# Graph attention layer on one core: the last two x products behind their s, the first R row from a TensorE product, four adj pieces loaded early, the verdict from a bound

## What is computed

```python
Wh = x @ W.T                               # 8192 x 256
s_i = Wh @ r[:256, 0];  s_j = Wh @ r[256:, 0]
e = s_i[:, None] + s_j[None, :]            # 8192 x 8192
e = where(e >= 0, e, 0.2 * e)
e = where(adj == 0, -inf, e)
out = gelu(softmax(e, axis=1) @ Wh)        # exact gelu
return layernorm(x + out)                  # over the 256 features
```

## Time and profile before

| | us |
|---|---|
| median of three runs | 1577.04 |
| profiled execution | 1579.86 |
| its span in the trace | 1578.1 |
| PE busy | 1547.4 (98%) |
| DVE busy | 1482.8 (94%) |
| ACT busy | 1180.9 (75%) |
| POOL busy | 455.3 (29%) |
| mean granted clock of PE | 0.992 |

### The profile page before, as it was taken

The page is one execution under the profiler, slowest core; times in us unless marked ns, Lnnn a source line. Parts: engine busy times, 40 slices in busy tenths (PEclk is TensorE's granted clock), DMA queues, the critical chain, the costliest instruction groups (busy, mean ns, idle before and its releaser), DMA issues.

```text
span 1578.1 us, 37090 instructions
## 1 busy us (share of the span) xinstructions
PE 1547.4 (98%) x12693; PEld 1536.3 (97%) x12693; DVE 1482.8 (94%) x1853; ACT 1180.9 (75%) x1527; POOL 455.3 (29%) x660
## 2 busy tenths in 40 slices
PE   9969999999999999999999999999999999999996
PEld 8869999999999999999999999999999999999996
DVE  4789999999999999999999999999999999999996
ACT  5666687777777777877777777777777777777773
POOL 0022223332232323223232322333232233333220
PEclk9989999999999999999999999999999999999998
DMA  7466876958777696878768686877878687787860
GB/s 175 99 95 80 109 99 81 139 75 125 100 115 105 86 134 81 125 94 121 99 91 129 87 123 89 127 94 98 121 93 123 84 126 95 102 115 99 114 91 29
DMA packets 295267, 164.41 MB, mean 104 GB/s; under 512 B 12336, under 2 KB 291120, under 8 KB 295216
## 3 DMA queue, kind: packets, MB, share of 16 engines
q0 software_dynamic: 278976, 142.12, 68.5%
q1 hardware_dynamic: 16240, 21.80, 4.9%
HBM read 289.67 MB, written 8.42 MB: 189 GB/s over the span
## 4 chain that ended last, share of the span: by engine, by line
PE 95%; issue 3%; ACT 1%; DMA 0%; POOL 0%; POOLq 0%; DVE 0%; ACTq 0%
PE acc L653 30%; PE acc L643 30%; PE acc L646 30%; PE acc L616 3%; PE acc L604 1%; ACT gates L341 0%; PE acc L582 0%; DMA R_row<-w_rows 0%; ACT P_hi L417 0%; ACT WV_hi L335 0%; DMA w_rows<-w_in 0%; POOL adj_in L249 0%; PE acc L592 0%; POOL rstd L286 0%; POOLq L58 0%
## 5 line engine op out<-in xcount | busy, mean ns | idle before, releaser
L643 PE MATMUL acc<-WV_hi,P_hi 128*128 (+1 forms) x4096 | 999.0, 282 | 9.8 <-ACT P_hi L417 9.7
L646 PE MATMUL acc<-WV_lo,P_hi 128*128 (+1 forms) x4096 | 998.1, 281 | 0.0
L643 PEld LDWEIGHTS acc<-WV_hi,P_hi 128*128 128x128 f32 x4096 | 774.8, 189 | 10.5 <-ACT P_hi L417 10.2
L417 ACT CAST P_hi<-Pw 128x1024 fp32r<-128x1024 f32 x512 | 537.5, 1050 | 316.4 <-DVE Pw L501 163.1
L646 PEld LDWEIGHTS acc<-WV_lo,P_hi 128*128 128x128 f32 x4096 | 772.8, 189 | 0.0
L501 DVE SCALAR_TENSOR_TENSOR Pw<-R_row,X,gatesT 128x512 f32<-128x512 f32 x1024 | 711.5, 749 | 2.8 <-DMA R_row<-w_rows 2.8
L511 DVE TENSOR_TENSOR P_lo<-Pw,P_hi 128x1024 fp32r<-128x1024 f32 x512 | 626.7, 1224 | 41.3 <-ACT P_hi L417 39.0
L249 POOL DMA_DIRECT2D adj_in<-in_adj x512 | 330.6, 653 | 873.9 <-ACT gates L341 820.1
L653 PE MATMUL acc<-WV_hi,P_lo 128*128 (+1 forms) x4096 | 575.7, 283 | 0.0
L341 ACT ACTIVATE gates<-adj_in 128x1024 uint8<-128x1024 bf16 x512 | 537.4, 1050 | 34.5 <-DMA adj_in<-in_adj 26.5
L653 PEld LDWEIGHTS acc<-WV_hi,P_lo 128*128 128x128 f32 x4096 | 527.1, 189 | 0.0
(11 more groups left out here) (63 smaller groups left out, 200.8 us busy)
## 6 DMA issues: line engine op xcount, KB each, us to landing
adj_in<-in_adj POOLq DMA_DIRECT2D x512, 256.0 KB, 5.2
out<-y SPq DMA_DIRECT2D x64, 128.0 KB, 6.1
y<-in_x POOLq DMA_DIRECT2D x60, 128.0 KB, 5.9
Pw<-in_x SPq DMA_DIRECT2D x48, 128.0 KB, 3.6
R_row<-w_rows SPq DMA_DIRECT2D x16, 256.0 KB, 6.5
x_res<-in_x SPq DMA_DIRECT2D x20, 128.0 KB, 2.7
w_in<-in_L_gnn_W SPq DMA_DIRECT2D x1, 256.0 KB, 3.2
w_rows<-w_in SPq DMA_DIRECT2D x1, 32.0 KB, 2.1
```

The lines of the kernel that those rows point to most:

```text
L417: nc.scalar.copy(P_hi[:, u % 2], Pw[u][:]).then_inc(s_hi, 1)
L643: nc.tensor.matmul(acc[r_][:, v, 0:HC], P_hi[:, u % 2, par, bass.ts(v, P)], WV_hi[:, k, :], start=(first and u == 0 and par == 0), stop=False)
L646: nc.tensor.matmul(acc[r_][:, v, 0:FOUT], P_hi[:, u % 2, par, bass.ts(v, P)], WV_lo[:, k, :], start=False, stop=False)
```

## The change

The first stage does 30 whole products (0 to 29) and all 32 transposes. Of the rows 30 and 31 PE first computes only the two columns of s (`s_product`, a product of 2 columns instead of 258) and later the 256 columns of Wh (`late_product`). ACT takes V of these from S, and makes their `WV_hi` after the factor R (two parts) and within the first two groups (two parts). DVE makes their `WV_lo` in pieces 1 to 4 of the first row block, and the last column of `WV_hi` in piece 5; PE waits for them before the block's last piece.

The first R row isn't read back from DRAM. DVE multiplies the 32 x 32 unit matrix by s_i of the first 512 rows (`spread`, 32 x 512), PE multiplies this by a 32 x 128 tile of ones, which puts the row s_i on all partitions, DVE cuts it at `neg_M` out of PSUM, and ACT takes its exponential. The rows for the other blocks go through DRAM as before, and the first of them to be loaded is that of the second block.

POOL issues the loads of pieces 0 and 1 earlier (at `s_xT` 4 and 8), and those of pieces 2 and 3 still in the x stage, when the first and the second piece are gated. ACT gates pieces 0 and 1 in the x stage (after products 8, 10, ... 22), and nothing in the first piece of the main stage. DVE transposes the first piece's gates after product 18.

The verdict takes the largest |Wh| from products 0 to 27, and for the rest a bound: the largest |x| of the last two loads times the sum of |W| per output. It moves from DVE to POOL (a second partition reduction and ten small instructions). `applies` runs the main stage first and waits for the flag behind it; the general path still reads the flag.

The diff, cut to its core:

```diff
...
+        red = sb("red", [P, 6])
+        top = sb("top", [P, 6])
+        x_max = sb("x_max", [P, 2])
...
-        fits = sb("fits", [P, 5])
+        fits = sb("fits", [P, 6])
...
+        ones = y[0:32, 0, 0:P]
+        spread = y[0:32, 2:4, :].rearrange("p u (g n) -> p (u g) n", n=32)
+        ps_s = [acc[0][:, j, 0:4] for j in range(2)]
+        ps_row = acc[0][:, 0, :]
+        ps_Rt = acc[0][0:NC, 1, 0:P]
...
+            body()
             eng.wait_ge(s_flag, 1)
-            flag = eng.value_load(taken[0:1, 0:1], min_val=0, max_val=1)
-            with eng.If(flag == 1):
-                body()
...
-            load_rows(0, 0)
-            sp.wait_ge(s_Rld[0], 16)
...
-            pool.wait_ge(s_xT, 10)
+            pool.wait_ge(s_xT, 4)
             load(0, 0, 0, 0)
-            pool.wait_ge(s_xT, 18)
+            pool.wait_ge(s_xT, 8)
             load(0, 0, 0, 1)
-            pool.wait_ge(s_red, 2)
-            nc.gpsimd.partition_all_reduce(top[:, 0:2], red[:, 0:2], P, REDUCE_MAX).then_inc(s_top, 1)
-            pool.wait_ge(s_red, 3)
-            nc.gpsimd.partition_all_reduce(top[:, 2:3], red[:, 2:3], P, REDUCE_MAX).then_inc(s_top, 1)
+            pool.wait_ge(s_gate, GP)
+            load(0, 0, 1, 0)
+            pool.wait_ge(s_gate, 2 * GP)
+            load(0, 0, 1, 1)
+            pool.wait_ge(s_red, 4)
+            nc.gpsimd.partition_all_reduce(top[:, 0:1], red[:, 0:1], P, REDUCE_MAX).then_inc(s_top, 1)
+            pool.wait_ge(s_red, 5)
+            nc.gpsimd.partition_all_reduce(top[:, 1:6], red[:, 1:6], P, REDUCE_MAX).then_inc(s_fit, 1)
+            pool.wait_ge(s_fit, 1)
+            nc.gpsimd.tensor_scalar(fits[:, 0:1], top[:, 0:1], top[:, 1:2], MAX_SPREAD, ALU.add, ALU.is_le).then_inc(s_fit, 1)
+            nc.gpsimd.tensor_scalar(fits[:, 1:3], top[:, 0:2], MAX_S, None, ALU.is_le).then_inc(s_fit, 1)
+            nc.gpsimd.tensor_scalar(fits[:, 3:4], top[:, 2:3], MAX_WH, None, ALU.is_le).then_inc(s_fit, 1)
+            nc.gpsimd.tensor_scalar(fits[:, 4:6], top[:, 4:6], top[:, 3:4], MAX_WH, ALU.mult, ALU.is_le).then_inc(s_fit, 1)
+            pool.wait_ge(s_fit, 5)
+            for q in range(1, 6):
+                nc.gpsimd.tensor_tensor(fits[:, 0:1], fits[:, 0:1], fits[:, q:q + 1], ALU.mult).then_inc(s_fit, 1)
+                pool.wait_ge(s_fit, 5 + q)
+            nc.gpsimd.tensor_copy(taken[0:1, 0:1], fits[0:1, 0:1]).then_inc(s_flag, 1)
...
-                block_loads(0, 0, first=2, before=False)
+                block_loads(0, 0, first=4, before=False)
...
+            def high_part(j, between=None):
...
+                    if between and r_ == 0:
+                        between()
...
+            def late_high_part(k):
+                nc.scalar.activation(WV_hi[:, k, 0:FOUT], ps_wh[(k // 2) % 3][:, k % 2, 0:FOUT], ACT.Copy,
+                                     scale=V[:, k:k + 1]).then_inc(s_hi0, 1)
...
-            for j in range(NP):
-                high_part(j)
-                if j + 2 < NP:
+            for j in range(NP - 2):
+                if j < NP - 3:
+                    high_part(j)
                     copy_x(j + 2)
-                if NP - 4 < j:
-                    if j == NP - 3:
+                else:
+                    high_part(j, between=lambda: copy_x(NP - 1))
+                if j >= 8 and j % 2 == 0 and j < 24:
+                    if j == 8:
                         act.wait_ge(s_adj[0], 64)
-                    gate(0, j - (NP - 3))
-            nc.scalar.copy(WV_hi[:, :, FOUT], V[:]).then_inc(s_vh, 1)
-
-            gate(0, GP - 1)
-            act.wait_ge(s_adj[1], 64)
+                    if j == 16:
+                        act.wait_ge(s_adj[1], 64)
+                    gate((j - 8) // 8, (j - 8) // 2 % GP)
+            act.wait_ge(s_v, NP - 2)
+            nc.scalar.copy(WV_hi[:, 0:NC - 4, FOUT], V[:, 0:NC - 4]).then_inc(s_vh, 1)
+            act.wait_ge(s_s, NP)
+            nc.scalar.activation(V[:, NC - 4:NC], S[:, NC - 4:NC, 1], ACT.Exp, scale=ALPHA).then_inc(s_v, 1)
+            act.wait_ge(s_v, NP - 1)
+            nc.scalar.copy(WV_hi[:, NC - 4:NC, FOUT], V[:, NC - 4:NC]).then_inc(s_vh, 1)
+            act.wait_ge(s_dve, 2)
+            nc.scalar.activation(X[:], S[:, :, 1], ACT.Exp, bias=shift[:], scale=1.0 - ALPHA).then_inc(s_X, 1)
+            act.wait_ge(s_rcut, 1)
+            nc.scalar.activation(R_row[:, 0, :], R_row[:, 0, :], ACT.Exp, bias=shift[:], scale=ALPHA - 1.0).then_inc(s_R0, 1)
...
-            nc.scalar.activation(X[:], S[:, :, 1], ACT.Exp, bias=shift[:], scale=1.0 - ALPHA)
+            act.wait_ge(s_wh, NP - 1)
+            late_high_part(NC - 4)
+            late_high_part(NC - 3)
             act.wait_ge(s_Rt, 1)
-            nc.scalar.copy(Rt, acc[0][0:NC, 0, 0:P]).then_inc(s_Rtc, 1)
+            nc.scalar.copy(Rt, ps_Rt).then_inc(s_Rtc, 1)
...
+                        ahead = not (last and c == PC - 1) and (before or c > 0)
...
+                            if not before and c == 0 and u < 2:
+                                if u == 0:
+                                    act.wait_ge(s_wh, NP)
+                                late_high_part(NC - 2 + u)
...
+            def copy_late_s(j):
+
+                dve.wait_ge(s_s2, j - (NP - 2) + 1)
+                nc.vector.tensor_copy(S[:, 2 * j:2 * j + 2, :], ps_s[j % 2].rearrange("p (r c) -> p r c", c=2)).then_inc(s_s, 1)
+            def low_part_of(k):
...
+            def x_maximum(n):
+                dve.wait_ge(s_x[n % 4], 64 * (n // 4 + 1))
+                nc.vector.tensor_reduce(x_max[:, n - 14:n - 13], x_in[n % 4], AX.XY, ALU.max,
+                                        apply_absolute_value=True).then_inc(s_xm, 1)
+
+            dve.wait_ge(s_w, 16)
+            nc.vector.tensor_reduce(red[:, 4:6], w_in[:], AX.X, ALU.add, apply_absolute_value=True).then_inc(s_red, 1)
+            for j in range(NP - 3):
+                low_part_of(2 * j)
+                low_part_of(2 * j + 1)
                 copy_s(j)
-                wh_maximum(j)
-            copy_s(NP - 1)
+                if j < NP - 4:
+                    wh_maximum(j)
+                if j == 18:
+                    transpose_piece(0, 0)
+                if j == 24 or j == 26:
+                    x_maximum(2 + j // 2)
+                if j == NP - 4:
+                    dve.wait_ge(s_max, NP - 4)
+                    nc.vector.tensor_reduce(red[:, 2:3], wh_max[:, 0:2 * (NP - 4)], AX.X, ALU.max).then_inc(s_red, 1)
+                    dve.wait_ge(s_xm, 2)
+                    nc.vector.tensor_tensor(red[:, 3:4], x_max[:, 0:1], x_max[:, 1:2], ALU.max).then_inc(s_red, 1)
+            low_part_of(2 * (NP - 3))
+            copy_s(NP - 3)
+            copy_late_s(NP - 2)
+            dve.wait_ge(s_s, NP - 1)
+            row_s = S[0:32, :, 0].rearrange("p (g e) -> p g e", e=4)[:, :, 0:1]
+            nc.vector.tensor_tensor(spread, ident[0:32, 0:32].unsqueeze(1).to_broadcast([32, 16, 32]),
+                                    row_s.to_broadcast([32, 16, 32]), ALU.mult).then_inc(s_dg, 1)
+            copy_late_s(NP - 1)
...
+            low_part_of(2 * (NP - 3) + 1)
             dve.wait_ge(s_top, 1)
             nc.vector.tensor_scalar(neg_M[:], top[:, 0:1], -1.0, None, ALU.mult).then_inc(s_dve, 1)
             nc.vector.tensor_scalar(shift[:], top[:, 0:1], -1.0, LEVEL, ALU.mult, ALU.add).then_inc(s_dve, 1)
             dve.wait_ge(s_dve, 2)
+            dve.wait_ge(s_row, 1)
+            nc.vector.tensor_scalar(R_row[:, 0, :], ps_row, neg_M[:], None, ALU.max).then_inc(s_rcut, 1)
             nc.vector.tensor_scalar(s_i_cut[:], S[:, :, 0], neg_M[:], None, ALU.max).then_inc(s_cut, 1)
...
             dve.wait_ge(s_vh, 1)
-            nc.vector.tensor_tensor(WV_hi[:, :, FOUT + 1], V[:], WV_hi_read[:, :, FOUT], ALU.subtract).then_inc(s_vl, 1)
-
...
-            transpose_piece(0, 0)
+            nc.vector.tensor_tensor(WV_hi[:, 0:NC - 4, FOUT + 1], V[:, 0:NC - 4], WV_hi_read[:, 0:NC - 4, FOUT],
+                                    ALU.subtract).then_inc(s_vl, 1)
+            dve.wait_ge(s_X, 1)
...
+            def late_part(n):
+
+                if 1 <= n <= 4:
+                    low_part_of(NC - 5 + n)
+                if n == 5:
+                    dve.wait_ge(s_vh, 2)
+                    nc.vector.tensor_tensor(WV_hi[:, NC - 4:NC, FOUT + 1], V[:, NC - 4:NC],
+                                            WV_hi_read[:, NC - 4:NC, FOUT], ALU.subtract).then_inc(s_vl, 1)
...
+                        if late and u == 1:
+                            late_part(2 * cp + i)
...
+                    if not before:
+                        dve.wait_ge(s_R0, 1)
+                        for n in range(PC):
+                            piece(ah, r_, n // 2, n % 2, first=n == 0, late=True)
+                        return
+                    dve.wait_ge(s_Rld[r_], 16 * ah + 16 * r_)
...
-            for j in range(NP):
+            for j in range(NP - 2):
                 wh_product(j)
-                if j + 2 < NP:
```

(29 more changed lines are left out.)

46 lines of the change are left out of this document (16 added, 30 removed).

## The result

The changed kernel takes 1568.58 us (median of four runs, 1567.79 to 1570.87) beside 1577.26 for the kernel before on the same chip; the ratio is 0.9944, 95% interval 0.9932 to 0.9957. In a later comparison of the same two it was 1569.67 (six runs) beside 1577.83, ratio 0.9945 (0.9932 to 0.9958). The forecast was 1566.5, the range 1564.5 to 1570.8. The gain is there, 8.2 to 8.7 us instead of 10.5.

A forecast was written before the change was run, and what follows sets the result against it. PE holds 95% of the chain, so only the transition (12.4 + 2.0 us) could shrink: 8.6 from the start plus 2.0 from the clock, less 0.1, makes 10.5 us, 1577.04 to 1566.5; range 1564.5 to 1570.8.

The forecast's parts named there:

- Steps 1 to 7: Transition from product 29's end to the first main product at 83.15 instead of 91.76; start gains 8.6 us.
- step 7: End of transition: first weights at 80.55, P_hi at 82.0 level with ACT's queue at 82.05, PE starts 83.15.
- Step 8: First main-stage group: PE has no gap over 0.8 us, clock stays up, 2.86 instead of 4.88 us; gains 2.0.
- rival A: PE's clock falls in the transition's 2-column products; PE starts 3.6 late, first group up to 2.0 more, 1570.1 to 1572.1; chance 0.12.
- the 8.6 of the start: Gain forecast for the first main product's earlier start, at 83.15 instead of 91.76.
- B: Transition: the transposed R, not the row, comes last; 1567.5 with 1 us of delay; chance 0.06 for over 1.4 us.
- C: ACT's adj-piece wait at second block's end, costing PE 1.5 us, goes (1565.0) or comes elsewhere (1568.0); chance 0.09.
- D: DVE becomes the bound in the first block, 0.4 us in four pieces, 1568.0; chance 0.06.
- E: POOL's verdict, eleven instructions, delays the fifth piece's load; at 4 us each PE waits 13.5 us, 1580; chance 0.02.
- the 100 asked for: Sign to look for afterwards: POOL's verdict over before 100 us on the trace's time axis.
- What is put elsewhere: Gates, transpose, maxima and loads in the x stage covered; late low parts in the first block charged 0.1 us.

The follow-up runs named there:

- after_again: The changed kernel run once more, unchanged, for the spread; 1569.67 us, ratio 0.9945 to the kernel before.
- e3: Changed kernel, but every engine waits for the verdict's flag, reads it and branches before the main stage, as before the change; 1577.96 us, ratio 1.0000.
- e7: Changed kernel with late product 30's first half ahead of the row product and first P_hi rounded before the late high parts and transposed-R copy; 1569.44 us, ratio 0.9938.
- e8: e6 with product 30 whole in its old place and only product 31 late; 1570.83 us, ratio 0.9952 to the kernel before.
- before_again: The kernel before, unchanged, run for a second trace; 1578.59 us, one run.
- e4: Changed kernel, but adj pieces 0 and 1 load later, 2 and 3 behind the verdict, the second piece gated in the main stage; 1577.20 us, ratio 0.9999.
- e6: Changed kernel, but ACT rounds the first P_hi before the late high parts and the transposed-R copy, whose PSUM moves to another accumulator; 1569.52 us, ratio 0.9945.
- e1: Changed kernel, but the first R row goes through DRAM again, stored and loaded back; 1575.41 us, ratio 0.9988 to the kernel before.
- e5: Changed kernel, but the first half of late product 30 stands ahead of the row product; 1569.59 us, ratio 0.9947 to the kernel before.
- e2: Changed kernel, but products 30 and 31 are multiplied whole in their old place; 1569.82 us, ratio 0.9947 to the kernel before.
- e9: The kernel before with only the row product on PE for the first R row, nothing else of the change; 1576.99 us, ratio 0.9983.

## Why the prediction was right, and where its size was off

**Steps 1 to 7, right as long as the clock holds.** Counted from the end of product 29, as predicted and as in the changed kernel and after_again: spread 1.5, measured 1.6 and 1.6; row seen by DVE 3.3, measured 3.7 and 3.6; `neg_M` 3.1, measured 3.15 both; first weights 4.8, measured 5.3 and 5.2; first main product 7.4, measured 9.3 and 7.7. The row product took 1.05 us from its start to the next row instead of 0.87 (1.16 where the clock fell in it), the cut 0.75 instead of 0.68 and 0.72 was right for the exponential. The level of step 7, weights plus 1.45 against ACT's queue, is exact in after_again, where both stand at 83.9.

**Step 8, the step that failed.** "PE has no gap over 0.8 us now" was true and not enough: the clock fell in the changed kernel although PE had not waited more than 0.3 us before it. With it step 7's late products, three at 0.87 us each, came out at 4.23 us instead of 2.61. That is rival A, given 0.12. Of the eight traces with a thin stretch and the row product behind it, six show the fall within the products (the changed kernel, e3 to e7), e8 has it behind a short wait, and after_again not at all. Rival A was priced at 3.6 us and up to 2.0 more. It cost 1.6, since the clock was back at 80.2, within the late products, and the first group came out at 2.98 us. So the 2.0 us of step 8 were gained nearly whole, and 1.6 of the 8.6 of the start were lost. Forecast 10.5; with 1.6 off it is 8.9, beside 8.64 at the fifth group and 8.2 to 8.7 between the medians. That this fits so well is in part luck: with the clock held (after_again) 10.22 us stood at the fifth group, and 8.9 to 10.0 were left at the end of the spans. Single waits and the start move each execution by as much as the term in question. The time came into the range because the range was wide enough for part of A, not because step 8 went as written.

**B** was level as forecast; where the clock fell, it was what set the end (ACT 1.57 us in front of the late high parts). **C** was right in kind: the wait comes and goes. It is 1.5 us at 266 in the kernel before and none in before_again, none in the changed kernel and 1.15 at 1449 in after_again, and the variants have none or one of 0.9 to 1.6 us, at several places (apart from the 5.7 us that e4's late loads cost). It can't be credited to the change. **D** didn't occur: PE waits nowhere in the first block. **E** was harmless, but not for the reason given. POOL's first verdict instruction came 6.7 us after the reductions, which no step had, and the ten instructions then took 6.1 us (83.81 to 89.89) (9.8 in after_again), where eleven were priced at 16.6. The end, 89.9, was within the 100 asked for, and 97.35 in after_again nearly used it up. In the ten traces with the verdict on POOL that gap lies between 6.70 and 7.31 us.

The Trainium skill (GPSIMD Engine Reference, Instruction dispatch) tells of about 6 us, with no instruction to see, at the first call of freshly loaded code. The gaps here are of that size; no trace shows that they are such a load.

The rule of the Trainium skill (GPSIMD Engine Reference, Key points) that POOL contends with DVE instructions of two SBUF inputs, weighed in the prediction, agrees with what is measured. A product of POOL took 0.25 us with DVE idle (e3), and also in e6, where DVE only transposed gates and waited. It took 0.56 us on average in the changed kernel, mostly beside L586 and L576, and up to 0.78 in the variants (e1).

**What is put elsewhere** was covered: PE's distance from product to product is 2.18 us in both kernels (12.47 to 14.65, before 12.38 to 14.56), with no wait in the x stage behind the first product. That product 29 ends at 73.63, 77.30 or, in the kernel before, 75.73 and 75.39, is decided by some 14 us.

**What the parts are worth together.** Undone one at a time, by the traces, the row product costs 6.5 us, the late products 1.7, the flag behind the stage 9.3 and the early loads 8.2, which is 25.7 for a gain of 8.6; the row product alone gives 2.0. (The 8.2 is taken at the sixth group.) They stand in series behind one another's cover, and none has a price of its own. What decides whether the clock falls in the thin stretch stays open: the same program does both, filling the gap (e5) didn't help, and shortening the stretch (e8) put the fall later. Neither of its two parts went with a fall by itself. Behind the 2-column products alone the late products ran at full rate (e1), and the row product behind whole products had the clock at 1.00 (e2 and e9, where it fell only in a later wait). These are single traces, and the program with both parts held the clock once too. No version that was run beats the changed kernel by more than its medians scatter.

## What to carry to other kernels

When several short chains end at one point, remove the longest on paper and read what stands at the point then, and go on until the next bound is real work; measure the whole set, and then each part undone, since a part may turn out to bring no time (here the late products). That PE has no gap isn't enough to count on its clock: here it fell in a stretch of narrow products without one. So price what follows such a stretch at both levels, and see whether the work behind it leaves time for the clock to be back before the stage that matters. Count times from a common event in both traces (here the end of product 29), since the start of a program can differ by several us from one execution to the next.

## What the runs showed of the hardware

- The granted clock went from 2.4 to 1.2 GHz at 76.8 us in the changed kernel, with no wait over 0.3 us. Before it PE had done 16 rows of 2 columns in 2.0 us and was in a product of 32 partitions; it was back at 80.2, within the late products. In after_again it stayed at 2.4 GHz through the same work.
- The start of the program is uneven. The first whole product began between 8.00 and 9.49 us and product 29 ended between 73.6 and 77.3, in the old order and the new. The granted clock is recorded at 0.50 from 8 to 11 us in before_again and in e7. In after_again and the first trace of before it is recorded at 1.00 although the rows run at half rate (in after_again four transposes take 1.06 us, 0.60 later). The Trainium skill (TensorE: Matmul & The Clock Gate, What's actually happening) says that the number of slow matmuls at the start differs from run to run; these traces agree.
- From the end of two partition reductions on POOL to its next ordinary instruction 6.7 to 7.3 us pass, also with DVE idle (6.77 in e3). A DMA issue behind one came after 2.16 us in the kernel before, the wait for the flag included.
